# Attention of image 1: values in four column groups, denominators summed on GpSimd, and four smaller edits

## The reference

```python
x = x + _L0_conv_ref(_gn(x), ...)   # deformable 3x3 convolution with mask, batch norm, relu
x = x + _L1_conv_ref(_gn(x), ...)   # 1x1 products with sign/tanh estimates
x = x + _L2_conv_ref(_gn(x), ...)   # deformable 3x3 convolution (offsets from a 3x3 convolution)
x = x + _L3_conv_ref(_gn(x), ...)   # attention over all pixels
# _L3_conv_ref, N = 4096 pixels, 32 channels:
f1, f2, f3 = (einsum('oc,bcn->bon', w_k, xf) + b_k for k in 1, 2, 3)
A = softmax(einsum('bcn,bcm->bnm', f1, f2), axis=-1)
out = einsum('bcm,bnm->bcn', f3, A) + xf
```

## Time and profile before

| | |
|---|---|
| median of three runs | 1315.96 us |
| profiled execution, whole | 1317.74 us |
| its span, first to last instruction | 1315.0 us |
| TensorE, VectorE, ScalarE, GpSimd busy | 1166.4, 1011.4, 661.8, 484.8 us |
| mean granted TensorE clock | 0.945 of full speed |

### The profile page before, as it was taken

How to read it: one execution, slowest core, us unless ns; L and a number is a source line. 1 busy time by engine, 2 the same in 40 slices (tenths; PEclk the granted TensorE clock), 3 DMA queues, 4 the chain that set the end, 5 groups by cost and what they waited for, 6 DMA issues and landing times.

```text
span 1315.0 us, 20260 instructions
## 1 busy us (share of the span) xinstructions
PE 1166.4 (89%) x7066; PEld 490.1 (37%) x7126; DVE 1011.4 (77%) x1679; ACT 661.8 (50%) x882; POOL 484.8 (37%) x537
## 2 busy tenths in 40 slices
PE   4899997586999999978898888888998999999996
PEld 1788884143444443422232322222222222222221
DVE  8799998894766566668879888888766777777772
ACT  4877675644554455322343444444655444444453
POOL 4000000037777777777777777772000000000000
PEclk9999997697999999956799999999999999999999
DMA  2654450048544442111111111110000000000000
GB/s 53 138 131 112 120 103 1 0 127 234 157 124 131 140 151 69 52 47 49 51 54 50 52 51 51 50 50 22 1 1 1 8 9 0 0 0 0 0 1 16
DMA packets 59672, 79.21 MB, mean 60 GB/s; under 512 B 12230, under 2 KB 43974, under 8 KB 59414
## 3 DMA queue, kind: packets, MB, share of 16 engines
q1 hardware_dynamic: 44342, 47.03, 13.6%
q0 software_dynamic: 15264, 31.29, 8.4%
HBM read 70.94 MB, written 7.34 MB: 60 GB/s over the span
## 4 chain that ended last, share of the span: by engine, by line
PE 67%; DVE 21%; issue 5%; ACT 4%; DMA 1%; DVEq 1%; SPq 0%; ACTq 0%; another core or an unknown queue 0%
PE psum L1831 15%; PE psum L1966 12%; PE psum L1948 9%; PE psum L1989 8%; PE psum L1716 6%; DVE maxes L1143 5%; DVE quads L372 3%; PE psum L1731 3%; DVE probs_and_weighted L881 3%; PE psum L1914 3%; PE psum L1743 2%; PE psum L1841 2%; PE psum L1803 2%; PE psum L1995 2%; DVE probs_and_weighted L891 2%
## 5 line engine op out<-in xcount | busy, mean ns | idle before, releaser
L554 POOL DMA_INDIRECT tile_data<-quad_table,index_u x477 | 470.0, 985 | 409.2 <-DMA quad_table<-quad_rows_or_splits 260.7
L1143 DVE TENSOR_REDUCE maxes<-psum 128x1 f32<-128x512 f32 x512 | 329.1, 683 | 98.9 <-PE psum L1948 92.1
L1573 ACT ACTIVATE quads<-psum 128x1024 f32<-128x1024 f32 x256 | 248.1, 1021 | 260.7 <-PE psum L1995 241.5
L1966 PE MATMUL psum<-quads 128*64 128x512 f32 x1024 | 267.0, 616 | 7.1 <-DVE maxes L1143 6.9
L1831 PE MATMUL psum<-scratch,quad_rows_or_splits 128*128 128x512 f32 (+1 forms) x486 | 209.1, 571 | 20.8 <-DVE scratch L966 19.2
L1989 PE MATMUL psum<-quads,probs_and_weighted 32*128 32x512 f32 x1024 | 146.9, 643 | 3.5 <-issue 2.1
L1831 PEld LDWEIGHTS psum<-scratch,quad_rows_or_splits 128*128 128x128 f32 x486 | 87.8, 192 | 117.1 <-issue 101.2
L1948 PE MATMUL psum<-products_or_attention 128*128 128x512 bf16 x226 | 83.8, 414 | 42.6 <-DVE maxes L1143 37.5
L978 DVE TENSOR_TENSOR probs_and_weighted<-psum,quads 128x512 f32<-128x512 f32 (+1 forms) x81 | 51.5, 643 | 79.3 <-PE psum L1831 74.1
L1432 ACT ACTIVATE vals<-psum 96x384 f32<-96x384 f32 x53 | 25.8, 487 | 144.3 <-PE psum L1795 144.3
L1966 PEld LDWEIGHTS psum<-quads 128*64 128x64 f32 x1024 | 55.4, 136 | 107.2 <-issue 100.0
(11 more groups left out here) (226 smaller groups left out, 1431.3 us busy)
## 6 DMA issues: line engine op xcount, KB each, us to landing
products_or_attention<-positions SPq DMA_DIRECT2D x30, 576.0 KB, 8.0
products_or_attention<-bands SPq DMA_DIRECT2D x12, 768.0 KB, 7.6
tile_data<-quad_table,index_u POOLq DMA_INDIRECT x477
quads<-bands SPq DMA_DIRECT2D x6, 768.0 KB, 10.7
quad_table<-quad_rows_or_splits SPq DMA_DIRECT2D x4, 768.0 KB, 9.1
products_or_attention<-bands SPq DMA_DIRECT2D x4, 576.0 KB, 8.4
quad_table<-quad_rows_or_splits SPq DMA_DIRECT2D x2, 640.0 KB, 8.5
products_or_attention<-positions SPq DMA_DIRECT2D x4, 288.0 KB, 6.8
```

The costliest lines, as they stand in the source:

```text
L554: pool.indirect_dma_start(out=out[:, k * CORNERS * C:(k + 1) * CORNERS * C], out_offset=None, in_=table, in_offset=bass.IndirectOffsetOnAx ...
L1143: v.reduce_max(maxes[:, c // NBLK, c % NBLK:c % NBLK + 1], psum[:, FREE + c % 2, :], AXIS_X)\
L1573: act.activation(probs[:, s % 2, 2 * BLK * h:2 * BLK * (h + 1)], psum[:, SCORES + 2 * h:SCORES + 2 * h + 2, :].rearrange("p a n -> p (a n) ...
L1966: last = pe.matmul(psum[2 * C * h:2 * C * h + 2 * C, SUMS, :], f3[b][:, 4 * s + i, :], probs[:, s % 2, BLK * i:BLK * i + BLK], start=s == ...
```

## The change

**Attention of image 1.** weigh multiplies by 32 columns of values alone, the four tiles of a quad into the four 32-partition groups of bank SUMS, after both exponentials of the quad are done. GpSimd adds the quad's probabilities, two tiles to two (128 x 1024, into pair_sums), then these (128 x 512, into quad_sums[s]); ScalarE's exponentials of quad s wait for the first of these additions of quad s-2. TensorE multiplies quad_sums by ones in four column groups of bank TOTALS (bank 7), quads 0 to 3 in quad 5 (early) and 4 to 7 in quad 1 of the next block (late). ScalarE copies SUMS and TOTALS after the exponentials of quads 0 and 2, TensorE adds their four groups in quad 3 (stack_groups: stationary is four identity blocks), ScalarE copies the result after quad 4, and VectorE takes reciprocals, quotient and addition in quads 5, 6 and 7, ahead of that quad's maxima and, in quad 7, ahead of take_queries and negated. The queries' fill is made in quad 7 as for image 0, and the chunks are cut as two before weigh and the rest behind it. After the last quad of all, late totals, stacking and the quotient follow.

**Besides.** TOP becomes 34 (halves of 34 and 30 rows, in layers 0 and 2); ScalarE loads the Sqrt table before take_sums of layer 1; the first tile's weights are copied before the hats, after a wait for image 0's indices only; stack has a fourth identity block.

```diff
 SCORES, SUMS, FREE, SAMPLES = 0, 4, 5, 7
+TOTALS = SAMPLES
...
         conv_rep = sb("conv_rep", [P, TAPS, C])
-        stack = sb("stack", [3 * C, C])
+        stack = sb("stack", [4 * C, C])
...
         packed_values = scratch[:, 6 * BLK:8 * BLK].rearrange("p (m n) -> p m n", n=P)
+        att_groups = scratch[:, 4 * BLK:6 * BLK].rearrange("p (k n) -> p k n", k=2)
+        pair_sums = work[:, 4 * BLK:6 * BLK]
+        quad_sums = tile_data[:, N // 2:N // 2 + KEY_QUADS * BLK].rearrange("p (s n) -> p s n", s=KEY_QUADS)
...
         scored = sem("scores_ready"); probs_ready = sem("probs_ready"); summed = sem("sums_done")
...
             if isinstance(n, tuple):
-                return SAMPLES if b else FREE + 1
+                return FREE + 1
...
         tile_weights = psum[:, SAMPLES, 3 * P:3 * P + TAPS * CORNERS]
-        TOP = H // 2 + 1
+        TOP = H // 2 + 2
...
             return b, (j[0], j[1], j[2] - 1)
+        def has_totals(b, j):
+            return b == 1 and not (isinstance(j[0], int) and j[2] == 0)
...
                         gather(quad_table[1][b], gathered[:, n % SLOTS, :], n % SLOTS, gathers[n % SLOTS])
+            def sum_probs(j):
+                var, stp, start = j
+                for s in range(KEY_QUADS):
+                    p = (var, KEY_QUADS * stp, KEY_QUADS * start + s)
+                    pool.wait_ge(probs_ready, lin(p, 2, 2 * KEY_QUADS * NBLK + 2))
+                    wait(pool, quads_summed, lin(p))
+                    pool.tensor_tensor(pair_sums, probs[:, s % 2, 0:2 * BLK], probs[:, s % 2, 2 * BLK:4 * BLK], ALU.add)\
+                        .then_inc(probs_paired, 1)
+                    pool.wait_ge(probs_paired, lin(p, 1, 1))
+                    wait(pool, totals_made, lin(j, 2, 0 if s >= 4 else -1))
+                    pool.tensor_tensor(quad_sums[:, s, :], pair_sums[:, 0:BLK], pair_sums[:, BLK:2 * BLK], ALU.add)\
+                        .then_inc(quads_summed, 1)
+            pool.wait_ge(outs_read, sum(GATHERED))
+            sum_probs((0, 0, 0))
+            with pool.Fori(1, NBLK) as j:
+                sum_probs((j, 1, 0))
...
                     .then_inc(bands_made, 1)
-                for q in range(3):
+                for q in range(4):
...
                     v.tensor_tensor(x_of[b][:, here], x_of[b][:, here], quotient, ALU.add).then_inc(x_final, 1)
+            def quotient_part(b, j, k):
+                var, stp, start = j
+                total, inverse, quotient = att_sum[:, 0, :], att_sum[0:C, 1, :], att_sum[IMAGE[b], 2, :]
+                if k <= 4:
+                    v.wait_ge(stacks_copied, lin(j, 1, 1))
+                    part_of = slice(P * (k - 1), P * k)
+                    v.reciprocal(inverse[:, part_of], att_sum[C:2 * C, 0, part_of]).then_inc(quotient_steps, 1)
+                elif k == 5:
+                    v.wait_ge(quotient_steps, lin(j, 5, 4))
+                    v.tensor_tensor(quotient, total[0:C, :], inverse, ALU.mult).then_inc(quotient_steps, 1)
+                else:
+                    v.wait_ge(quotient_steps, lin(j, 5, 5))
+                    at = lin(j, BLK)
+                    here = slice(at, at + BLK) if isinstance(at, int) else bass.ds(at, BLK)
+                    v.tensor_tensor(x_of[b][:, here], x_of[b][:, here], quotient, ALU.add).then_inc(x_final, 1)
...
                 var, stp, start = j
+                totalled = has_totals(b, j)
...
                         sum_corners(1, *merged_pair(j, s // 2))
+                    for k in {5: (1, 2), 6: (3, 4), 7: (5, 6)}.get(s, ()) if totalled else ():
+                        quotient_part(*before(b, j), k)
...
                         negated(b_next, nxt)
-                    if s and not first:
+                    if s and not first and not totalled:
                         sum_part(*before(b, j), s - 1)
-                    if ahead and s == (3 if b else KEY_QUADS - 1):
+                    if ahead and s == KEY_QUADS - 1:
...
                     attend(b, (0, 0, NBLK - 1), last=True)
-                    for k in range(7):
-                        sum_part(b, (0, 0, NBLK - 1), k)
+                    for k in range(1, 7):
+                        quotient_part(b, (0, 0, NBLK - 1), k)
...
                 act.wait_ge(rows_copied, 9 * B)
+                act.wait_ge(indexed, 1)
+                take_weights(0).then_inc(first_weights, 1)
...
                 hats_of_bands(1, 0)
-                act.wait_ge(indexed, B)
-                take_weights(0).then_inc(first_weights, 1)
...
                 act.activation(att_halves[:, 1, :], psum[2 * C:4 * C, SUMS, :], ACT.Identity).then_inc(sums_copied, 1)
+            def copy_groups(j):
+                var, stp, start = j
+                act.wait_ge(sum_steps, SUM_STEPS * NBLK)
+                act.wait_ge(summed, lin((var, stp, start + NBLK), KEY_QUADS, KEY_QUADS))
+                act.activation(att_groups[:, 0, :], psum[:, SUMS, :], ACT.Identity).then_inc(sums_copied, 1)
+            def copy_totals(j):
+                act.wait_ge(totals_made, lin(j, 2, 2))
+                act.activation(att_groups[:, 1, :], psum[:, TOTALS, :], ACT.Identity).then_inc(totals_copied, 1)
+            def copy_stacks(j):
+                act.wait_ge(stacked, lin(j, 1, 1))
+                act.activation(att_sum[:, 0, :], psum[0:2 * C, TOTALS, :], ACT.Identity).then_inc(stacks_copied, 1)
...
                 var, stp, start = j
+                totalled = has_totals(b, j)
...
                     wait(act, summed, lin(n, 1, -1))
+                    if b:
+                        wait(act, probs_paired, lin((var, KEY_QUADS * stp, KEY_QUADS * start + s), 1, -1))
...
                                        ACT.Exp).then_inc(probs_ready, 1)
-                    if s == 0 and not first:
+                    if s == 0 and not first and not totalled:
                         copy_sums(*before(b, j))
-                    if ahead and s == (2 if b else KEY_QUADS - 1):
+                    if totalled and s in (0, 2, 4):
+                        (copy_groups, copy_totals, copy_stacks)[s // 2](before(b, j)[1])
+                    if ahead and s == KEY_QUADS - 1:
...
                         attend(b, (0, 0, j), last=j == NBLK - 1)
-                    act.wait_ge(sum_steps, SUM_STEPS * (NBLK * B - 2) + 1)
-                    copy_sums(b, (0, 0, NBLK - 1))
+                    copy_groups((0, 0, NBLK - 1))
+                    copy_totals((0, 0, NBLK - 1))
+                    act.wait_ge(quotient_steps, 5 * (NBLK - 1))
+                    copy_stacks((0, 0, NBLK - 1))
...
                 l1_tanh_and_sign(b)
+            act.preload_act_table(ACT.Sqrt)
...
                 w = width(TAPS * i)
-                pe.matmul(psum[0:C, ADDED_BANK, 0:w], stack[:, :], conv_parts[:, 0:w], start=True, stop=True).then_inc(parts_added, 1)
+                pe.matmul(psum[0:C, ADDED_BANK, 0:w], stack[0:3 * C, :], conv_parts[:, 0:w], start=True, stop=True).then_inc(parts_added, 1)
...
                 pe.wait_ge(probs_ready, lin(n, 2, half + 1))
+                if b:
+                    for i in range(4) if half else ():
+                        last = pe.matmul(psum[C * i:C * i + C, SUMS, :], f3[b][:, 4 * s + i, 0:C],
+                                         probs[:, s % 2, BLK * i:BLK * i + BLK], start=s == 0, stop=s == KEY_QUADS - 1)
+                    if half:
+                        last.then_inc(summed, 1)
+                    return
...
                     last.then_inc(summed, 1)
+            def add_totals(j, late):
+                pe.wait_ge(quads_summed, lin(j, KEY_QUADS, 8 if late else 4))
+                for g in range(4):
+                    last = pe.matmul(psum[C * g:C * g + C, TOTALS, :], ones[:, 0:C], quad_sums[:, 4 * late + g, :],
+                                     start=not late, stop=bool(late))
+                last.then_inc(totals_made, 1)
+            def stack_groups(j):
+                var, stp, start = j
+                pe.wait_ge(sums_copied, lin((var, stp, start + NBLK), 1, 1))
+                pe.wait_ge(totals_copied, lin(j, 1, 1))
+                for k in range(2):
+                    last = pe.matmul(psum[C * k:C * k + C, TOTALS, :], stack[:, :], att_groups[:, k, :], start=True, stop=True)
+                last.then_inc(stacked, 1)
...
                 var, stp, start = j
+                totalled = has_totals(b, j)
...
                     ready = min(m, 2)
-                    half_way = ready if tiles and s % 2 == 0 else max(ready, m // 2 + ready // 2)
+                    half_way = ready if b or tiles and s % 2 == 0 else max(ready, m // 2 + ready // 2)
...
                     score_chunks(b_next, nxt, range(cuts[0], cuts[1]))
-                    if ahead and b == 0 and s == KEY_QUADS - 1:
-                        pe.wait_ge(maxed, lin((var, stp, start + 1), MAXIMA, MAXIMA))
+                    if ahead and s == KEY_QUADS - 1:
```

(13 more changed lines are left out.)

2 lines of the change are left out of this document (1 added, 1 removed).

## The result

1352.65 us median (1352.03 to 1354.94, 4 runs) against 1316.02 for the kernel before (1315.5 to 1316.31, 4 runs): ratio 1.0284, 95% interval 1.0267 to 1.03, slower by 37 us. The forecast said 1300 and a range of 1283 to 1339. The profiled execution has a span of 1350.3 us, before 1315.0.

The account below looks back on a forecast made before the run. TensorE was taken to set the pace, with VectorE late at many hand-overs. Other edits -10.5 and attention -5.1 made -15.6 on the median of 1315.96: 1300 us, range 1283 to 1339 (the forecast's own 1291 to 1310).

Parts of the forecast that it names:

- Early edits, -10.5: Ahead of image 1's attention: row split, Sqrt table and first weights moved save 10.5 us together, bounds -1 and -15.
- the rows: Image halves of 34 and 30 rows: faster writes save 3.0 us at one place and 1.2 at the kernel's start.
- the weights: First tile's weights copied ahead of the hats, so the first selection runs at once: -5.0 us, 6.1 at most.
- the table's share: Sqrt table loaded earlier, beside VectorE's statistics instead of just ahead of the deviation: -1.3 us.
- TensorE's part: Image 1's attention: eight products in 1.0 us, totals and stacking 1.0 each; five-chunk quads last 4.3, with stacking 5.3.
- GpSimd's durations: Image 1's attention: additions of 2.2 and 1.2 us, 3.8 a quad with idle gaps, fitting under 4.5.
- The step that failed: Quad 7 of image 1's blocks: quotient work ahead of the query copy moves the next row by 1.06, 3.84 becoming 4.9.
- Block 0, -4.7: Image 1's first block, without late totals or quotient: 33.1 us, counted as a saving of 4.7.
- Tail, +6.7: Block 7 and the end: GpSimd ends late, then totals, copies and stacking follow in 3.9 us; +6.7 us.
- Rival (1): Block boundaries of image 1: GpSimd's additions shut VectorE out, some 5 us at seven boundaries, 35 in all: 1335; chance 0.28.
- the forecast's blocks: Image 1's attention, predicted row-to-row lengths: 36.3 us against 37.8 in blocks 1 to 5, 33.1 in block 0.

Follow-up runs that it names:

- small_adds: The changed kernel with both GpSimd additions cut to 4 columns, leaving the denominators out: 1296.07 us, ratio 0.9866 to the kernel before.
- pe_busy: The changed kernel with 16 more unused products on TensorE ahead of its wait for image 1's negated maxima: 1342.76 us, ratio 1.0224 to the kernel before.
- direct_67: The changed kernel, TensorE instead of GpSimd summing quads 6 and 7, quotient behind the negated maxima, block 7 in the old form: 1297.11 us, ratio 0.9868.
- adds_held: The changed kernel, GpSimd waiting for the next block's negated maxima before adding quad 6's probabilities: 1311.5 us, ratio 0.997 to the kernel before.

## Why the prediction was wrong

- **Early edits, -10.5**: right as a sum, -10.7 at the first row of image 1 and -11.9 alone, and in part by luck: the rows gave twice their share, the weights a little less, and the table's share doesn't show. What was forecast of the single places came: ten writes took 15.3 us instead of 24.3 (1.42 each for 34 rows, 1.47 forecast), the first product came at 295.04, gathers ended at 888.9.
- **TensorE's part**: right. Eight column-group products take 1.06 us, totals 1.04 to 1.06, stacking 1.05; scores start 4.32 us apart in five-chunk quads, 5.30 with the stacking.
- **GpSimd's durations**: right. 2.34 and 1.27 us, 3.7 a quad with the gap, for 2.2, 1.2 and 3.8.
- **The step that failed** is "the copy of the queries starts at 2.6 instead of 1.54 and all behind it, negated maxima, their transposition, their row, moves by 1.06: 3.84 becomes 4.9". It priced VectorE's boundary at the durations that its operations had beside an idle GpSimd. 9.8 was measured, and 5.0 without the additions' length. In small_adds the gaps sum to 258.1 instead of 301.5: 43 us, 6.2 a boundary, of which pe_busy puts 8 to 13 in all down to the clock. The forecast has no term for the clock either.
- **Block 0, -4.7**: block 0 had never been 37.8, it was 41.7 before, so the level of 33.1 was wrong. As a difference -4.7 is near what came without the collision (37.05 with the additions held, 37.75 in small_adds), which is luck; the changed kernel itself has 41.1.
- **Tail, +6.7**: +11.1. The last addition ends at 1335.74, 6.3 us behind the last exponentials, as worked out. Then totals and stacking ran at half clock, 1.93 and 1.92 instead of 1.06 and 1.05, and from the addition's end to the reciprocals it is 5.4 us for the 3.9 forecast; the rest is block 7's slow beginning.
- **Rival (1)** had the mechanism, the place and nearly the price, "some 5 us at each of seven boundaries", and 0.28. A boundary of the changed kernel lasts 4.8 us longer from scores to scores than one of small_adds. It was short by 17 us of 1352, about the sum of the clock behind the idles (8 to 13), the tail (4.4) and what even small_adds took above the forecast's blocks (3.3). Its evidence against, "no row shows VectorE waiting for GpSimd", was no evidence: in the kernel before GpSimd was idle through image 1's attention. The range's top of 1339 added no second cost to the first.

What decided was something new running beside a chain of short dependent operations. That chain was in the trace, and so was one blocked gather.

## What to carry to other kernels

Before giving GpSimd a share of the work, list VectorE's operations with SBUF operands that stand on the path beside it. Each of them, however small, can cost the rest of one GpSimd operation: here four of nine did. So price a hand-over by GpSimd's operations that fall into it and not by the lengths of VectorE's. Put GpSimd's work beside PSUM-reading maxima and reciprocals, where it was free here, and give the stretch around a hand-over to another engine (direct_67) rather than delay the work (adds_held). Then price TensorE's halved clock behind every idle that this makes.
